# Who makes the input of each scan step: seven of sixteen by ScalarE, six by VectorE, three by GpSimd

## The chip, the core and the metric

The kernel runs on one core of a Trainium2 chip. A core has TensorE (matrix products and transposes, in the profile PE, its weight loads PEld), VectorE (DVE), ScalarE (ACT), GpSimd (POOL) and SyncE (SP, which here issues most DMAs). Each engine works through its own list of instructions in order, and semaphores tie the lists together. The metric is device microseconds (us) of one execution; lower is better. The time before is the median of three runs.

## The reference: what is computed

The input is `x` (4 images, 32 x 32 positions, 384 channels, float32). One block of a state space model with a mixture of experts behind it:

- `x` is normalised over channels and projected to `xh` and `z` (192 channels each); `xh` goes through a 3 x 3 depthwise convolution and SiLU.
- A selective scan runs over the 1024 positions in four directions `k` (rows, columns, both also backwards), for each of 16 states `n`:

```
dA = exp(d_t[..., None] * As)
h  = h * dA + (d_t * u_t)[..., None] * B_t[:, :, None, :]
y  = sum over n of h * C_t
```

- The four results are added, normalised, gated by `silu(z)`, projected back to 384 channels and added to `x`.
- Each token then goes through the one of 8 experts that its gate picks, and that result is added too.

The change is in the scan alone.

## The kernel before, in words

**Two passes.** The four images are handled as two pairs, one pass (`p`) each; partitions 0 to 63 hold one image of the pair, 64 to 127 the other, and the 192 channels lie in `CG` = 3 blocks `j`. A pass is: projection and convolution, the time steps `delta` and their products `du`, the scan, then norm, gate and output projection. The experts come after both passes.

**The scan.** A pass has `STEPS` = 128 steps: 4 directions, 2 halves of 512 positions, 16 states. Sixteen steps with one direction and one half are called a group here (8 groups a pass, g = 0 to 7), and a step is named by its state number n = 0 to 15 in its group. In even groups the recurrence starts from zero ("first half"); in odd groups ("second half") it starts from the state kept by the first half, which VectorE reads as a column. A step needs five things:

1. Its *input* `du * B` (128 x 1536, to a slot of the ring `X3` with `RING` = 7 slots). The letter `MAKER[n]` says who makes it. **P**: GpSimd, by one multiplication (L464). **D**: VectorE, by one multiplication that reads `du` from PSUM (L913), issued one step ahead: `input_of(s + 1)` stands before `scans(s)`. **A**: ScalarE scales the transposed `du` by columns of B, in eight small *scalings* (L683, 128 x 192 each, `scale_duT`), and TensorE transposes the result block by block into PSUM (L1273, `transpose_input`). When the eight scalings are issued is the table `SCALED`: the key is the step in which ScalarE issues them, `(m, f, l)` means scalings f to l - 1 of state m.
2. Its *decay* `exp(delta * A)`, three ScalarE instructions `exp(s, j)`. For a P or D step they go to one of only two PSUM banks `dA` (L706), taken in turn, so each waits until the scan before the last one has ended. For an A step they go to SBUF (L701, `dAs`), and the two banks hold the transposed input instead.
3. Three *scans* on VectorE (L937), one for each j.
4. The product with C on GpSimd (L479, in place in `X3`), which releases `s_hc`.
5. The sum over n on TensorE (L1247, `add_up`, three matrix products of 128 x 512 into PSUM), which frees the slot of `X3`. The first step of a group also opens the sums (L1236, `open_sums`), and for that the sums of the group before must have been taken away by ScalarE: `y_out` (L723 as one instruction, or L727 as three that also turn the block). It stands in step n = 2 of the next group.

**Order on ScalarE.** This is written out by hand, and the same for both kernels. In step s:

```python
exp(s, 0)
exp(s, 1)
...
if MAKER[n] == "A" or n % 2:
    exp(s, 2)
...
for m, f, l in todo:
    if m < STEPS:
        scale_duT(m, f, l)
if n == 2 and g:
    y_out(g - 1)
if not (MAKER[n] == "A" or n % 2):
    exp(s, 2)
```

So scalings and `y_out` stand in front of the third decay where n is even and the step is not A, and behind it otherwise. In first halves a 128 x 3 copy (L715, `keep_state`) is issued behind `exp(s, 1)` too. At n = 14 and 15 the `du` of the next group is copied out (L671, L691).

**Order on GpSimd.** In step s it makes the input of step s + 2 if that is a P step, and then multiplies step s by C.

**Loads.** SyncE loads the rows of B five steps ahead (for P and D steps only, ring of 4) and the rows of C six steps ahead (ring of 6). In step 4 x 16 of the first pass it also loads the next pass's images.

Of the kernel before, what the change touches and what calls it, by code (L numbers as in the profile page):

```python
# [10 lines left out]
ACT = mybir.ActivationFunctionType  # L11
AX_X = mybir.AxisListType.X

P = 128
NB, HH, WW, DM = 4, 32, 32, 384
L = HH * WW
DI, NS, R, ND = 192, 16, 24, 4
# [11 lines left out]
IN_ARENA = 5  # L29
RING, B_RING, C_RING = 7, 4, 6  # L30
GROUPS_OF_PAIR = 4 * 2
MAKER = "PDADPDADPDADPDAA"
BY_SCALAR = (2, 6, 10, 14, 15)
LAST_D = 13
SCALED = {15: ((2, 0, 3),), 0: ((2, 3, 8),), 2: ((6, 0, 2),), 4: ((6, 2, 8),), 6: ((10, 0, 5),),
          8: ((10, 5, 8), (14, 0, 3)), 10: ((14, 3, 8),), 12: ((15, 0, 6),), 13: ((15, 6, 8),)}
B_AHEAD = 5
LB = HALF // P
KORDER = (0, 2, 1, 3)
PREP = (0, 1, 2, 3)  # L40
# [9 lines left out]
def build(nc, x, w_in, conv_w, conv_b, w_xd, w_dt, bias_row, a_log, d_skip, ln_g, ln_b, w_out,  # L50
          w_gate, b_gate, w1, w2, w3, sel, ident_d, half_ones, tri_d, out):
    ctx = ExitStack()
    with ctx:
# [6 lines left out]
        def sems(*ns):  # L60
            return [sem(n) for n in ns]
# [68 lines left out]
        BT = carve(ND * TT * 2 * len(BY_SCALAR)).rearrange("p (k t b n) -> p k t b n", k=ND, t=TT, b=2)  # L130
# [44 lines left out]
        for at in (GL, xc_at):  # L175
# [76 lines left out]
        s_btps, s_bt, s_duTps, s_duT, s_scaled, s_dAs, s_inT = sems(  # L252
            "b_columns_in_psum", "b_columns_ready", "duT_in_psum", "duT_ready", "scaled_ready",
            "dA_in_sbuf", "input_in_psum")
# [22 lines left out]
        STEPS = ND * 2 * NS  # L277
# [6 lines left out]
        def inputs_before(c, maker):  # L284

            return c // NS * MAKER.count(maker) + MAKER[:c % NS].count(maker)

# [10 lines left out]
        def _(sp):  # L298
# [18 lines left out]
            for p in range(PAIRS):  # L317
# [30 lines left out]
                def load_b(s):  # L348
                    r = rows_before(STEPS * p + s)
                    before = [q for q in range(s) if MAKER[q % NS] != "A"]  # L350
                    if len(before) >= B_RING:
# [79 lines left out]
        def _(g):  # L431
# [5 lines left out]
            for p in range(PAIRS):  # L437
# [17 lines left out]
                def input_of(s):  # L455

                    _, gr, _, n, _ = place(s)
                    c = STEPS * p + s
                    g.wait_ge(s_steps[gr % 2], 32 * (GROUPS_OF_PAIR // 2 * p + gr // 2 + 1))
                    r = rows_before(c)  # L460
                    g.wait_ge(s_b[r % B_RING], 32 * (r // B_RING + 1))
                    if c >= RING:
                        g.wait_ge(s_xfree, c - RING + 1)
                    g.tensor_tensor(X3[c % RING], steps[gr % 2][1], Bs[r % B_RING][:, None, :].to_broadcast([P, CG, HALF]),  # L464
                                    ALU.mult).then_inc(s_dbp, 1)

                for s in range(STEPS):
                    kk, _, _, n, first = place(s)
                    c = STEPS * p + s
                    if s == 0:  # L470
                        input_of(0)
                    if s + 2 < STEPS and MAKER[(s + 2) % NS] == "P":
                        input_of(s + 2)
                    g.wait_ge(s_c[c % C_RING], 32 * (c // C_RING + 1))
                    g.wait_ge(s_scan, CG * (c + 1))
                    if first:
                        g.wait_ge(s_state, states_before(c + 1))
                    x = X3[c % RING]
                    g.tensor_tensor(x, x, Cs[c % C_RING][:, None, :].to_broadcast([P, CG, HALF]), ALU.mult)\  # L479
                     .then_inc(s_hc, 1)  # L480
# [53 lines left out]
        def _(a):  # L534
# [73 lines left out]
            for p in range(PAIRS):  # L608
# [7 lines left out]
                def b_columns(i):  # L616
                    c, cols = ND * p + i, bank[0].rearrange("p (t b n) -> p t b n", t=TT, b=4)[:, :, 0:2, :]
                    a.wait_ge(s_btps, c + 1)
                    a.activation(BT[:, PREP[i], :, :, 0:4], cols[:, :, :, 2:15:4], ACT.Copy)
                    a.activation(BT[:, PREP[i], :, :, 4], cols[:, :, :, 15], ACT.Copy).then_inc(s_bt, 1)  # L620

                if p:
                    a.wait_ge(s_tst, 16 * 2 * GROUPS)
# [900 lines left out]
```

## Time and profile before

| | |
|---|---|
| median of 3 runs | 1888.18 us (1885.74 to 1891.11) |
| the profiled execution | 1891.21 us, its span 1889.4 us |
| busy share of the span | PE 82%, PEld 40%, DVE 77%, ACT 57%, POOL 69% |
| scan of the first pass | 148.3 to about 710 us |
| scan of the second pass | 903.3 to about 1459 us |
| granted TensorE clock, mean | 0.918 |

The span is that from the first to the last instruction. Busy shares are means over stages that have different limits: in the two scan stretches VectorE and GpSimd are both nearly always busy, in the experts behind 1555 us TensorE is. A busy time of a group of instructions is the sum of their durations. Instructions of an engine overlap a little at their ends, so the distance from one start to the next (called the pitch below) is shorter than the duration.

### The profile page before, as it was taken

To read this page: it belongs to the slowest core of one execution; us is meant where nothing else is said; L and a number is where in the kernel's file an instruction comes from. 1 tells how busy PE (TensorE), PEld (TensorE's weight loads), DVE (VectorE), ACT (ScalarE), POOL (GpSimd) and SP (SyncE) were. 2 spreads that over 40 slices of the span, in tenths; PEclk is the share of its full clock that TensorE was granted. 3 is DMA by queue.
4 is the path that set the end of the run, shared out by engine and by line. 5 is a ranking of instruction groups with operands and counts; after the bars stand their busy time and mean duration, and the time that the engine had idled before them with its cause. 6 is when DMAs were issued, how large, how long until landed. Compare 5 with 4: busy or idle time off the path is not lost.

```text
span 1889.4 us, 17637 instructions
## 1 busy us (share of the span) xinstructions
PE 1542.0 (82%) x4977; PEld 764.8 (40%) x4978; DVE 1460.3 (77%) x1564; ACT 1080.5 (57%) x1959; POOL 1305.8 (69%) x498
## 2 busy tenths in 40 slices
PE   5866877886887887986688888888887659999997
PEld 2323433433433433442244344344343345555554
DVE  5588999998999997847899999999997762333322
ACT  3777777776777764657777777776775211111110
POOL 1458999998999992414899999999998112222222
PEclk9877999998999888987899999988999869999999
DMA  3184435436434312028443543443433471111110
GB/s 120 45 295 177 126 115 174 132 101 211 125 110 139 103 55 90 35 95 280 177 131 109 175 133 99 145 139 93 136 106 103 178 280 43 42 42 47 50 50 18
DMA packets 107232, 227.96 MB, mean 121 GB/s; under 512 B 18222, under 2 KB 31057, under 8 KB 103312
## 3 DMA queue, kind: packets, MB, share of 16 engines
q1 hardware_dynamic: 102160, 213.02, 34.3%
q0 software_dynamic: 4992, 14.01, 2.4%
q8 instruction: 33, 0.54, 0.1%
q14 instruction: 47, 0.39, 0.1%
HBM read 183.93 MB, written 44.40 MB: 121 GB/s over the span
## 4 chain that ended last, share of the span: by engine, by line
PE 33%; DVE 28%; POOL 18%; issue 13%; ACT 4%; DMA 3%; SPq 1%; DVEq 0%; POOLq 0%; ACTq 0%
DVE arena L937 18%; POOL arena L479 14%; PE psum L1400 10%; PE psum L1419 5%; DVE arena L913 4%; PE psum L1247 3%; PE psum L1220 2%; PE psum L1150 2%; POOL arena L464 2%; DMA arena<-bc_dram 2%; PE psum L1273 2%; PE psum L1326 1%; PE psum L1182 1%; PE psum L1345 1%; POOL arena L446 1%
## 5 line engine op out<-in xcount | busy, mean ns | idle before, releaser
L479 POOL TENSOR_TENSOR arena<-arena 128x1536 f32<-128x1536 f32 x256 | 875.8, 3452 | 31.7 <-ACT arena L715 19.1
L1247 PE MATMUL psum<-arena,ident 128*128 128x512 f32 x1536 | 742.0, 620 | 67.0 <-POOL arena L479 66.9
L937 DVE TENSOR_TENSOR_SCAN arena<-psum,arena 128x512 f32<-128x512 f32 x528 | 614.9, 1231 | 0.0
L706 ACT ACTIVATE psum<-arena 128x512 f32<-128x512 f32 x528 | 364.2, 690 | 271.0 <-DVE arena L937 259.1
L1247 PEld LDWEIGHTS psum<-arena,ident 128*128 128x128 f32 x1536 | 283.1, 198 | 371.0 <-issue 251.4
L937 DVE TENSOR_TENSOR_SCAN arena<-arena,psum 128x512 f32<-128x512 f32 x240 | 289.3, 1240 | 24.9 <-PE psum L1273 20.1
L1273 PE MATMUL psum<-ident,arena 128*128 128x128 f32 x960 | 159.8, 295 | 151.4 <-DVE arena L937 151.4
L1273 PEld LDWEIGHTS psum<-ident,arena 128*128 128x128 f32 x960 | 122.0, 151 | 289.1 <-issue 147.4
L683 ACT ACTIVATE arena<-arena 128x192 f32<-128x192 f32 x640 | 234.6, 440 | 0.0
L464 POOL TENSOR_TENSOR arena<-arena 128x1536 f32<-128x1536 f32 x64 | 220.6, 3447 | 4.5 <-issue 4.5
L913 DVE TENSOR_TENSOR arena<-psum,arena 128x1536 f32<-128x1536 f32 x112 | 194.2, 1734 | 24.0 <-ACT psum L691 13.8
L1400 PE MATMUL psum<-arena 128*128 x468 | 197.9, 560 | 0.0
L796 ACT ACTIVATE arena<-psum 128x384 f32<-128x384 f32 x39 | 19.1, 490 | 294.3 <-PE psum L1391 294.3
L701 ACT ACTIVATE arena<-arena 128x512 f32<-128x512 f32 x240 | 160.1, 709 | 10.5 <-DVE arena L937 9.9
L453 POOL TENSOR_TENSOR arena<-arena 128x1024 f32<-128x1024 f32 x24 | 63.1, 2627 | 133.1 <-DVE arena L900 133.1
L516 POOL TENSOR_TENSOR gap<-one 128x1 f32<-128x1 f32 x39 | 11.5, 296 | 206.1 <-DVE arena L1100 206.1
L1083 DVE TENSOR_TENSOR arena<-arena,psum 128x469 f32<-128x469 f32 x39 | 25.1, 644 | 120.0 <-ACT arena L801 111.1
L1400 PEld LDWEIGHTS psum<-arena 128*128 128x128 f32 x468 | 86.4, 191 | 74.9 <-issue 65.0
L1419 PE MATMUL psum<-arena 128*128 (+1 forms) x312 | 107.3, 487 | 1.0 <-DVE arena L1090 1.0
L895 DVE SCALAR_TENSOR_TENSOR arena<-arena 128x1024 f32<-128x1024 f32 x24 | 43.2, 1799 | 54.7 <-ACT arena L641 54.5
L1220 PE MATMUL psum<-arena 64*128 64x512 f32 x96 | 62.7, 800 | 20.4 <-ACT arena L632 18.6
L446 POOL TENSOR_TENSOR arena<-arena 128x1024 f32<-128x1024 f32 x16 | 38.0, 2374 | 55.6 <-ACT arena L576 53.6
(161 smaller groups left out, 1464.2 us busy)
## 6 DMA issues: line engine op xcount, KB each, us to landing
arena<-bc_dram SPq DMA_DIRECT2D x864, 128.0 KB, 3.0
step_dram<-arena SPq DMA_DIRECT2D x16, 1536.0 KB, 8.1
arena<-step_dram SPq DMA_DIRECT2D x32, 768.0 KB, 8.0
arena<-in_x SPq DMA_DIRECT2D x8, 1536.0 KB, 9.4
arena<-in_w SPq DMA_DIRECT2D x6, 1876.0 KB, 10.7
t_dram<-arena SPq DMA_DIRECT2D x16, 386.0 KB, 3.8
arena<-in_w SPq DMA_DIRECT2D x4, 1536.0 KB, 13.6
z_dram<-arena SPq DMA_DIRECT2D x2, 1536.0 KB, 5.2
```

The lines of the kernel that those rows point to most:

```text
L464: g.tensor_tensor(X3[c % RING], steps[gr % 2][1], Bs[r % B_RING][:, None, :].to_broadcast([P, CG, HALF]), ALU.mult).then_inc(s_dbp, 1)
L479: g.tensor_tensor(x, x, Cs[c % C_RING][:, None, :].to_broadcast([P, CG, HALF]), ALU.mult)\
L683: a.activation(blocks(scaled[index % 2])[:, :, k, b, :], blocks(duT)[:, :, k, b, :], ACT.Copy, scale=BT[:, kk, LB * half + k, b, BY_SCALAR ...
L701: a.activation(dAs[j], steps[g % 2][0][:, j, :], ACT.Exp, scale=A[:, KORDER[kk], j, n:n + 1]).then_inc(s_dAs, 1)
L706: a.activation(dA[e % 2], steps[g % 2][0][:, j, :], ACT.Exp, scale=A[:, KORDER[kk], j, n:n + 1]).then_inc(s_dA, 1)
L913: v.tensor_tensor(X3[c % RING], dups, Bs[r % B_RING][:, None, :].to_broadcast([P, CG, HALF]), ALU.mult).then_inc(s_dbv, 1)
L937: v.tensor_tensor_scan(x, decay, given, 0.0 if first else state[:, n, j:j + 1], ALU.mult, ALU.add).then_inc(s_scan, 1)
L1220: ins = pe.matmul(bank[2 + 2 * j + h], wdt[0:64, KORDER[PREP[i]], j, :], xd[i % 2][0:64, h * HALF:(h + 1) * HALF], start=True, stop=True)
L1247: ins = pe.matmul(bank[j], ident[:, :], X3[c % RING][:, j, :], start=False, stop=(n == NS - 1), skip_group_check=True)
L1273: ins = pe.transpose(dA[e % 2][:, k * P:(k + 1) * P], scaled[index % 2][:, at:at + P], ident[:, :])
L1400: ins = pe.matmul(bk[:, 0:F], xsT[u][:, k, :], w[:, k, bass.ds(e * F, F)], start=(k == 0), stop=(k == KC - 1))
L1419: ins = pe.matmul(bank[6 + u][:, 0:DM], hidT[u][0:m, k, :], W3[0:m, k, bass.ds(e * DM, DM)], start=(k == 0), stop=(k == FC - 1))
```

## The change

The string that says who makes each input, the table of ScalarE's scalings and the step in which GpSimd begins its inputs:

```diff
-MAKER = "PDADPDADPDADPDAA"
-BY_SCALAR = (2, 6, 10, 14, 15)
+MAKER = "PDDADADAPADAPDAA"
+BY_SCALAR = (3, 5, 7, 9, 11, 14, 15)
 LAST_D = 13
-SCALED = {15: ((2, 0, 3),), 0: ((2, 3, 8),), 2: ((6, 0, 2),), 4: ((6, 2, 8),), 6: ((10, 0, 5),),
-          8: ((10, 5, 8), (14, 0, 3)), 10: ((14, 3, 8),), 12: ((15, 0, 6),), 13: ((15, 6, 8),)}
+SCALED = {15: ((3, 0, 3),), 0: ((3, 3, 8),), 1: ((5, 0, 8),), 4: ((7, 0, 3),), 5: ((7, 3, 8),),
+          6: ((9, 0, 3),), 7: ((9, 3, 6),), 8: ((9, 6, 8),), 9: ((11, 0, 7),), 10: ((11, 7, 8), (14, 0, 2)),
+          11: ((14, 2, 5),), 12: ((14, 5, 8), (15, 0, 4)), 13: ((15, 4, 8),)}
@@ (GpSimd)
-                    if s + 2 < STEPS and MAKER[(s + 2) % NS] == "P":
-                        input_of(s + 2)
+                    if s + 3 < STEPS and MAKER[(s + 3) % NS] == "P":
+                        input_of(s + 3)
@@ (ScalarE, columns of B for the A steps)
-                    a.activation(BT[:, PREP[i], :, :, 0:4], cols[:, :, :, 2:15:4], ACT.Copy)
-                    a.activation(BT[:, PREP[i], :, :, 4], cols[:, :, :, 15], ACT.Copy).then_inc(s_bt, 1)
+                    a.activation(BT[:, PREP[i], :, :, 0:5], cols[:, :, :, 3:12:2], ACT.Copy)
+                    a.activation(BT[:, PREP[i], :, :, 5:7], cols[:, :, :, 14:16], ACT.Copy).then_inc(s_bt, 1)
```

In a group of 16 steps there were 4 P, 7 D and 5 A steps; now there are 3 P, 6 D and 7 A.

ScalarE's list, from the last step of group 0 to step 4 of group 1 (a second half). Before, L683 are the scalings, L706 the decays of P and D steps, L701 those of A steps, L723 is `y_out`:

```order
L683 ACTIVATE arena<-arena 128x3x64 x3
L706 ACTIVATE psum<-arena 128x512 x2
L715 ACTIVATE arena<-arena 128x3
L683 ACTIVATE arena<-arena 128x3x64 x5
L706 ACTIVATE psum<-arena 128x512 x4
L701 ACTIVATE arena<-arena 128x512 x3
L683 ACTIVATE arena<-arena 128x3x64 x2
L723 ACTIVATE arena<-psum 128x3x512
L706 ACTIVATE psum<-arena 128x512 x5
L683 ACTIVATE arena<-arena 128x3x64 x6
```

And in the change, where all these stand one line later in the file (L684 for L683, and so on):

```order
L684 ACTIVATE arena<-arena 128x3x64 x3
L707 ACTIVATE psum<-arena 128x512 x2
L716 ACTIVATE arena<-arena 128x3
L684 ACTIVATE arena<-arena 128x3x64 x5
L707 ACTIVATE psum<-arena 128x512 x4
L684 ACTIVATE arena<-arena 128x3x64 x8
L707 ACTIVATE psum<-arena 128x512 x2
L724 ACTIVATE arena<-psum 128x3x512
L707 ACTIVATE psum<-arena 128x512
L702 ACTIVATE arena<-arena 128x512 x3
L707 ACTIVATE psum<-arena 128x512 x2
L684 ACTIVATE arena<-arena 128x3x64 x3
```

Behind the last decay of step 1 there now stand eight scalings ahead of the first decay of step 2, `y_out` stands ahead of a decay of the same P or D step where it stood behind those of an A step, and in step 4 three scalings stand ahead of the last decay.

VectorE's list at the same place, from step 14 of group 0 on (order prints a scan as SCALAR_TENSOR_TENSOR; L937 are scans and L913 are inputs). Before:

```order
L937 SCALAR_TENSOR_TENSOR arena<-arena,psum 128x512 x6
L913 TENSOR_TENSOR arena<-psum,arena 128x1536
L937 SCALAR_TENSOR_TENSOR arena<-psum,arena 128x512 x6
L913 TENSOR_TENSOR arena<-psum,arena 128x1536
L937 SCALAR_TENSOR_TENSOR arena<-arena,psum 128x512 x3
L937 SCALAR_TENSOR_TENSOR arena<-psum,arena 128x512 x3
```

In the change:

```order
L938 SCALAR_TENSOR_TENSOR arena<-arena,psum 128x512 x6
L914 TENSOR_TENSOR arena<-psum,arena 128x1536
L938 SCALAR_TENSOR_TENSOR arena<-psum,arena 128x512 x3
L914 TENSOR_TENSOR arena<-psum,arena 128x1536
L938 SCALAR_TENSOR_TENSOR arena<-psum,arena 128x512 x6
L914 TENSOR_TENSOR arena<-psum,arena 128x1536
L938 SCALAR_TENSOR_TENSOR arena<-arena,psum 128x512 x3
```

The inputs of steps 1 and 2 now stand ahead of the scans of steps 0 and 1, and the scans of steps 1 and 2 follow one another with nothing between.

## Rows read from the trace of the kernel before

**Rows 1.** Chain that ended last, the page's line by source line.
```profile
DVE arena L937 18%; POOL arena L479 14%; PE psum L1400 10%; PE psum L1419 5%; DVE arena L913 4%; PE psum L1247 3%; PE psum L1220 2%; PE psum L1150 2%; POOL arena L464 2%; DMA arena<-bc_dram 2%; PE psum L1273 2%; PE psum L1326 1%; PE psum L1182 1%; PE psum L1345 1%; POOL arena L446 1%
```
**Rows 2.** Windows: the first pass's scan; length, then busy time of each engine.
```profile
148.30:707.00 558.70, 448.42 (x1365) 216.03 (x1366) 537.81 (x441) 408.67 (x794) 538.52 (x159) 0.94 0.40 128
```
**Rows 3.** Timeline of POOL: start, length, line, count.
```profile
548.02 13.73 POOL L479 TENSOR_TENSOR arena<-arena 128x1536 f32<-128x1536 f32 x4
561.71 3.45 POOL L464 TENSOR_TENSOR arena<-arena 128x1536 f32<-128x1536 f32 x1
```
**Rows 4.** Timeline of DVE, a first half, then a second half.
```profile
565.54 1.73 DVE L913 TENSOR_TENSOR arena<-psum,arena 128x1536 f32<-128x1536 f32 x1
567.19 6.79 DVE L937 TENSOR_TENSOR_SCAN arena<-psum,arena 128x512 f32<-128x512 f32 x6
573.89 1.73 DVE L913 TENSOR_TENSOR arena<-psum,arena 128x1536 f32<-128x1536 f32 x1
...
663.04 3.62 DVE L937 TENSOR_TENSOR_SCAN arena<-arena,psum 128x512 f32<-128x512 f32 x3
666.58 3.61 DVE L937 TENSOR_TENSOR_SCAN arena<-psum,arena 128x512 f32<-128x512 f32 x3
670.10 1.74 DVE L913 TENSOR_TENSOR arena<-psum,arena 128x1536 f32<-128x1536 f32 x1
```
**Rows 5.** Timeline of DVE: where groups begin, and the first pass's last scans.
```profile
216.10 1.73 DVE L913 TENSOR_TENSOR arena<-psum,arena 128x1536 f32<-128x1536 f32 x1
284.55 1.73 DVE L913 TENSOR_TENSOR arena<-psum,arena 128x1536 f32<-128x1536 f32 x1
701.64 5.17 DVE L937 TENSOR_TENSOR_SCAN arena<-arena,psum 128x512 f32<-128x512 f32 x4 [0.81 <-ACT arena L701]
903.31 1.76 DVE L913 TENSOR_TENSOR arena<-psum,arena 128x1536 f32<-128x1536 f32 x1 [7.66 <-ACT psum L691]
969.51 1.73 DVE L913 TENSOR_TENSOR arena<-psum,arena 128x1536 f32<-128x1536 f32 x1
```
**Rows 6.** What DVE's scans (L937), then its inputs (L913), waited for.
```profile
  PE psum L1273: 20.1, 21
  ACT arena L701: 1.9, 3
...
  issue: 10.2, 3
```
**Rows 7.** Timeline of ACT: chained decays, six scalings, decays again.
```profile
568.43 0.69 ACT L706 ACTIVATE psum<-arena 128x512 f32<-128x512 f32 x1 [0.32 <-DVE arena L937]
...
582.98 0.19 ACT L715 ACTIVATE arena<-arena 128x3 f32<-128x3 f32 x1
583.08 2.17 ACT L683 ACTIVATE arena<-arena 128x192 f32<-128x192 f32 x6
585.15 0.67 ACT L706 ACTIVATE psum<-arena 128x512 f32<-128x512 f32 x1
```
**Rows 8.** Timeline of ACT: step 13, two scalings, then step 14's decays; `y_out`.
```profile
431.96 2.83 ACT L727 ACTIVATE arena<-psum 128x512 f32<-128x512 f32 x3
434.59 0.69 ACT L706 ACTIVATE psum<-arena 128x512 f32<-128x512 f32 x1
...
555.83 0.69 ACT L706 ACTIVATE psum<-arena 128x512 f32<-128x512 f32 x1 [0.48 <-DVE arena L937]
556.46 0.79 ACT L683 ACTIVATE arena<-arena 128x192 f32<-128x192 f32 x2
557.15 1.93 ACT L701 ACTIVATE arena<-arena 128x512 f32<-128x512 f32 x3
...
575.43 1.43 ACT L723 ACTIVATE arena<-psum 128x1536 f32<-128x1536 f32 x1
700.87 0.72 ACT L701 ACTIVATE arena<-arena 128x512 f32<-128x512 f32 x1 [1.27 <-DVE arena L937]
```
**Rows 9.** The page's group of TensorE's transposes for A steps: busy, mean | idle before.
```profile
L1273 PE MATMUL psum<-ident,arena 128*128 128x128 f32 x960 | 159.8, 295 | 151.4 <-DVE arena L937 151.4
```

## The prediction

> **What bounds the kernel now.** I read the chain of waits first. Of the span, 18% lie on VectorE's scans, 14% on GpSimd's products with C and 4% on VectorE's inputs [rows 1]: the chain passes through the scan stage, changing between these two engines, and nothing outside that stage is touched by the change. The windows say how full they are: of the first pass's 558.7 us VectorE is busy 537.8, GpSimd 538.5, TensorE 448.4 and ScalarE 408.7 [rows 2]. Two engines at 96% are a tie, so I went to the timelines for the pitch of each.
>
> GpSimd: four products take 13.69 us from start to start [rows 3], 3.42 each, an input the same. A group has 16 + 4 of them, 68.4 us. VectorE: six scans take 6.70 us in a first half (1.117 each), three take 3.52 in a second half (1.175), and an input moves the next scan by 1.65 [rows 4]. Undisturbed groups last 66.2 us (first half, from 903.31 to 969.51) and 68.45 (second half, from 216.10 to 284.55) [rows 5]. So two groups are 134.65 us on VectorE and 136.8 on GpSimd: GpSimd is slightly the slower, falls behind, and what depends on it (TensorE's sums, behind which the transposes for A steps queue) then stops VectorE now and then. That is the 20.1 us of waits for transposes, with 1.9 for decays. Another 10.2 us are "issue" waits before VectorE's inputs [rows 6], where the list waits for rows of B; I leave these as they are, since SyncE still issues them five steps ahead.
>
> The third view is ScalarE's timeline, and it decides the forecast. It is busy only 73% of the stage, but it is in lockstep with VectorE: a decay for a P or D step may start only when the scan that used its bank has ended. The first scan starts at 567.19 and the next one 1.117 later at 568.31, and the decay starts at 568.43 [rows 4, 7]: 0.12 us behind the start of the following scan. A decay is 0.69 long, the next ScalarE instruction can start 0.63 behind its start [rows 8], and from the end of a late decay (700.87 + 0.72) to the scan that waited for it (701.64) are 0.05 us [rows 5, 8]. So a decay that starts at 0.12, ends at 0.81 and may be followed by its scan at 0.86 is due at 1.117: 0.26 us in hand, and no lead can be built up over P and D steps. What ScalarE does between two such decays is free only up to its gap.
>
> **The change, part by part.**
>
> *Removed.* One VectorE input a group: 16 groups x 1.65 = 26.4 us off VectorE. One GpSimd input a group: 16 x 3.42 = 54.7 us off GpSimd, which then needs 38 x 3.42 = 130.0 us for two groups, less than VectorE's 134.65 - 3.30 = 131.35 even with no stall. So GpSimd no longer falls behind, and the 22.0 us of waits [rows 6] mostly go: of 24 such waits I keep a tenth, 2 us. Beginning an input three steps ahead moves it in front of one product; with GpSimd faster than VectorE this is worth nothing. It reaches the slot of the ring freed by step s - 4, whose sum TensorE has made by then.
>
> *Added.* Two A steps a group. On TensorE 24 transposes, at their full 295 ns [rows 9] 7.1 us, where TensorE has (558.7 - 448.4) / 8 = 13.8 us idle: nothing. On ScalarE 16 scalings of 0.345 us (six in 2.07) [rows 7], 5.5 us a group, 88 us in all, while (558.7 - 408.7) / 8 = 18.8 us a group are idle. By the sum they fit. By their places they don't. Each place worked out, with zero at the scan start named, p = 1.117 in first halves and 1.175 in second halves, and `keep_state` costing 0.10 in first halves only [rows 7]:
>
> - **Step 1, eight scalings behind its third decay.** From the second scan of step 1: 0.12 + 0.63 + 8 x 0.345 + 0.69 + 0.05 = 4.25 us until step 2 can be scanned. VectorE is there after two scans, at 2.23 or 2.35, because the input of step 2 was already made ahead of the scans of step 1. Stall 2.02 or 1.90 us.
> - **Steps 4, 6, 10, three scalings between second and third decay.** From the step's first scan: 0.12 + 0.63 + (0.10) + 1.04 + 0.69 + 0.05 = 2.63 or 2.53, due at 2.23 or 2.35. Stall 0.40 or 0.18, three times. Before, every P or D step of even n had a VectorE input in front (1.65 more), so that six scalings fitted: 3.66 against 3.88; the row shows the decay straight behind its six, at 585.15 [rows 7]. Now an A step follows, and there is none.
> - **Step 8**, two scalings: 2.28 against 2.23, 0.05 in first halves. **Step 12**, seven, with an input in front: 4.01 against 3.88, 0.13 in first halves.
> - **Step 13, four behind the third decay**, ahead of step 14: 0.12 + 0.63 + 1.38 + 0.71 + 0.05 = 2.89, stall 0.66 or 0.54. With two scalings, as now, the same sum gives 2.20 and fits; the rows show those two between decay and decay [rows 8].
>
> That is 4.06 us in a first half and 2.98 in a second, 8 x 7.04 = 56.3 us.
>
> - **`y_out` in step 2.** It now lies ahead of the third decay of a D step. Continuing from the stall of step 1, the decays of step 2 start at 3.51 and 4.14, `y_out` at 4.77 (4.87). As one instruction it takes 1.37 (1.43 less the overlap), as three 2.63 (431.96 to 434.59) [rows 8]. The third decay then allows its scan at 6.88 (6.98) or 8.14 (8.24), due 4.25 + 2p = 6.60 (6.48). Stalls, g = 1 to 7: 0.28, 0.50, 1.54, 1.76, 0.28, 0.50, 1.54: 6.4 a pass, 12.8 us in all. The sums of the new group open behind it and step 3's transposes queue behind those, but the input of step 4 (1.65 us) covers that.
>
> *Sum.* 69.1 - 26.4 - 22.0 + 2.0 = +22.7 us. Against its own 1891.2 us the profiled execution would be 1913.9; it stands 3 us above the median of the runs, 1888.2, so I forecast **1911 us**.
>
> The Trainium skill ("Perfetto Trace Analysis", section "Optimizing Scalar/DVE Operations") says that with VectorE saturated, moving some of its work to ScalarE may pay; by busy shares alone that speaks for this change. It is the second rival below. The same page calls occupancy the way to find the engine to optimise; here the engine at 73% is the one that I expect to set the pace.
>
> **Rivals.**
>
> 1. *The busy sum holds (ends faster).* If ScalarE hid all its scalings, VectorE would be left with -26.4 and the waits for transposes with -20: 1888.2 - 46.4, about 1842 us. For it: 18.8 us idle a group against 5.5 added. Against it: that idle time is in pieces of 0.42 us behind each decay [rows 7] and longer ones at A steps. It decides where the stalls are under 46.4 / 16 = 2.9 us a group; I work out 4.3. Chance 0.08.
> 2. *Only the long bursts cost.* If the short ones at steps 4, 6, 8, 10, 12, 13 (56.3 - 8 x 3.92 = 25 us together) fall in slack that I have put too low, the sum is -2 us: 1886. Chance 0.12, about evenly faster and same.
> 3. *The waits for transposes stay.* With seven A steps VectorE depends on TensorE at 7 of 16 steps, and a sum issued ahead of a transpose still waits for GpSimd; keeping all 20 us gives 1931. Against it: GpSimd is the slack engine then. Chance 0.10.
> 4. *My forecast*, 1898 to 1925 by itself (the short stalls halved; or half the old waits kept). Chance 0.70.
>
> The range runs from between rival 2 and the baseline, 1886, to rival 3, 1931; outside are rival 1 and tails. No change within 0.3% (about 6 us, what a measurement of this kernel can tell) gets 0.09, faster 0.11, slower 0.80.
>
> **What the new profile would show.** VectorE waiting about 70 us for ScalarE's decays (L707, and L702 at step 14) where it now waits 1.9 for them; a gap of about 2 us ahead of the first scan of every step 2; a second one in that step, 0.3 to 1.8 us, from g = 1 on; groups of about 69 to 71 us; GpSimd with idle time in every group, waiting for scans. VectorE's inputs 96 instead of 112, GpSimd's 48 instead of 64, scalings 896 instead of 640. I am wrong if the first scan of step 2 follows step 1 without a gap, or if the waits for transposes are still near 20 us.

## The result

The change makes the kernel slower: 1965.13 us (median of 4 runs, 1964.41 to 1967.81) against 1886.96 us (4 runs, 1885.29 to 1891.11), a ratio of 1.042 [1.040, 1.043]. I had said slower, but 1911 us, range 1886 to 1931. The profiled execution took 1964.71 us with a span of 1962.8; before, the span was 1889.4. So 73.4 us have to be found.

The chain of the changed kernel, the page's line by source line, answers to [rows 1]:

```profile
DVE arena L938 27%; PE psum L1401 9%; PE psum L1420 5%; DVE arena L914 5%; ACT arena L684 4%; PE psum L1237 4%; PE psum L1248 3%; PE psum L1274 2%; PE psum L1221 2%; PE psum L1151 2%; ACT psum L707 2%; PE psum L1183 1%; PE psum L1327 1%; ACT arena L728 1%; PE psum L1346 1%
```

GpSimd's products, 14% of the chain before, have left it (all of GpSimd is 1% of it now). New are ScalarE's scalings (L684, 4%), its turned `y_out` (L728) and, what I had not expected, TensorE's opening products (L1237, 4%).

The page's groups of costly instructions; behind the bar busy time, mean ns of one, then idle time ahead of them with its main releaser:

```profile
L480 POOL TENSOR_TENSOR arena<-arena 128x1536 f32<-128x1536 f32 x256 | 875.9, 3454 | 166.8 <-ACT arena L716 90.3
L1248 PE MATMUL psum<-arena,ident 128*128 128x512 f32 x1536 | 740.3, 604 | 68.5 <-POOL arena L480 68.2
...
L684 ACT ACTIVATE arena<-arena 128x192 f32<-128x192 f32 x896 | 329.1, 440 | 0.0
L1274 PE MATMUL psum<-ident,arena 128*128 128x128 f32 x1344 | 207.9, 279 | 115.0 <-DVE arena L938 115.0
...
L914 DVE TENSOR_TENSOR arena<-psum,arena 128x1536 f32<-128x1536 f32 x96 | 166.3, 1732 | 15.0 <-ACT psum L692 15.0
L465 POOL TENSOR_TENSOR arena<-arena 128x1536 f32<-128x1536 f32 x48 | 165.8, 3455 | 0.0
```

The counts are those announced: 96 inputs by VectorE, 48 by GpSimd, 896 scalings. The second row holds what undid the forecast: `add_up` issues three products for each of 256 steps, 768 in all, and the profile has 1536 records of them. So a float32 product of 128 x 512 is **two** records in the profile (a record is one instruction as the trace lists it).

What VectorE's scans (L938) waited for, in us and times; it answers to [rows 6]:

```profile
  PE psum L1274: 72.2, 16
  ACT psum L707: 46.3, 50
  ACT arena L702: 9.8, 16
```

The waits for transposes went from 20.1 to 72.2 us, those for decays from 1.9 to 56.1; the 10.2 us of "issue" waits ahead of VectorE's inputs are gone (L914 still has 15.0 us of idle time, two waits at the start of a pass; L913 had the same two, 13.8 us, one of them in [rows 5]). With the 26.4 us of removed inputs that is 52.1 + 54.2 - 10.2 - 26.4 = 69.7 of the 73.4 us. Most of the rest lies in late scans that the rows count as busy time. In a second half of the change:

```profile
249.40 3.76 DVE L938 TENSOR_TENSOR_SCAN arena<-psum,arena 128x512 f32<-128x512 f32 x3
...
256.59 3.61 DVE L938 TENSOR_TENSOR_SCAN arena<-psum,arena 128x512 f32<-128x512 f32 x3
```

Step 6 has three scalings ahead of its last decay, step 8 two; step 6 is 0.15 us longer. Three such steps in 8 groups are 3.6 us.

Of the 72.2 us, 70.3 lie in 14 waits at one place, the first scan of step 3 in every group but the first of a pass. The timelines of VectorE, TensorE and ScalarE there, g = 1 (start, length, engine, line, count, in brackets the idle time before and what ended it; TensorE's last two rows are the same place in g = 2):

```profile
227.69 3.74 DVE L938 TENSOR_TENSOR_SCAN arena<-psum,arena 128x512 f32<-128x512 f32 x3 [1.88 <-ACT psum L707]
231.35 1.73 DVE L914 TENSOR_TENSOR arena<-psum,arena 128x1536 f32<-128x1536 f32 x1
...
236.99 3.62 DVE L938 TENSOR_TENSOR_SCAN arena<-arena,psum 128x512 f32<-128x512 f32 x3 [3.91 <-PE psum L1274]
```

```profile
229.59 4.25 PE L1237 MATMUL psum<-arena 128*128 128x512 f32 x6 [3.33 <-ACT arena L724]
...
233.68 2.74 PE L1248 MATMUL psum<-arena,ident 128*128 128x512 f32 x6
...
236.25 1.04 PE L1274 MATMUL psum<-ident,arena 128*128 128x128 f32 x8
...
303.18 5.00 PE L1237 MATMUL psum<-arena,ident 128*128 128x512 f32 x6 [4.72 <-ACT arena L724]
308.02 2.74 PE L1248 MATMUL psum<-arena,ident 128*128 128x512 f32 x6
```

```profile
224.12 2.86 ACT L684 ACTIVATE arena<-arena 128x192 f32<-128x192 f32 x8
...
226.88 1.28 ACT L707 ACTIVATE psum<-arena 128x512 f32<-128x512 f32 x2
...
228.11 1.43 ACT L724 ACTIVATE arena<-psum 128x1536 f32<-128x1536 f32 x1
```

Read them from below. The eight scalings hold up step 2's decays (VectorE waits 1.88), and `y_out` comes behind these. At its end, 229.5, TensorE may open the new sums (three products, six records), then it adds step 0 (three more), and only then, at 236.25, come the transposes for step 3. VectorE was ready at 231.35 + 1.73 = 233.08 and waits 3.91 us.

Two things make the queue long. The sums take 2.57 us for three products, 0.86 each (233.68 to 236.25), where I had reckoned 0.43. And the opening products take 4.09 (4.84 in g = 2), for the same number of the same size. The windows say why; columns are length, busy time of PE, PEld, DVE, ACT and POOL, granted clock, DMA share and GB/s:

```profile
229.60:231.60 2.00, 2.00 (x3) 0.97 (x4) 2.00 (x3) 2.00 (x4) 0.56 (x2) 0.50 0.68 140
303.20:308.00 4.80, 4.80 (x6) 2.02 (x7) 3.16 (x3) 2.59 (x5) 4.80 (x2) 0.55 0.92 323
308.00:311.00 3.00, 3.00 (x11) 1.50 (x10) 0.00 (x0) 0.00 (x0) 0.80 (x1) 1.00 0.97 312
```

TensorE had been idle for 3.33 us ahead of the first window (4.72 ahead of the second) and was granted half the clock, 1.2 GHz, for most of the opening products; for the sums behind them in g = 2 (the third window) it was back at 2.4 GHz.

The same sum can be made for each of the 14 places, from the starts in the three timelines. Six products at full clock (5.14 us) would leave waits of 2.38 to 2.73 us, 34.7 in all; the other 35.6 of the 70.3 us are time by which the queue was longer than that, the low clock. Three products' time, 2.57 us, would leave between -0.19 and 0.16, that is nothing.

The experiments were made from these rows. VectorE's scans and ScalarE's decays keep their line numbers in all that start from the changed kernel; TensorE's lines move by a few in some.

### The profile page after: what moved, and what is told of

The parts are those of the page before. It is cut to its first block, busy times and chain, and to the rows that moved or that the text cites. A ratio compares the mean times of both kernels' runs of the same rounds, so it can differ in the third digit from the quotient of the medians.

```text
span 1962.8 us, 18725 instructions
## 1 busy us (share of the span) xinstructions
PE 1590.3 (81%) x5361; PEld 781.5 (40%) x5362; DVE 1440.0 (73%) x1548; ACT 1150.8 (59%) x2215; POOL 1252.3 (64%) x482
## 4 chain that ended last, share of the span: by engine, by line
PE 37%; DVE 37%; ACT 12%; issue 12%; POOL 1%; DMA 1%; DVEq 0%; ACTq 0%; POOLq 0%
DVE arena L938 27%; PE psum L1401 9%; PE psum L1420 5%; DVE arena L914 5%; ACT arena L684 4%; PE psum L1237 4%; PE psum L1248 3%; PE psum L1274 2%; PE psum L1221 2%; PE psum L1151 2%; ACT psum L707 2%; PE psum L1183 1%; PE psum L1327 1%; ACT arena L728 1%; PE psum L1346 1%
## 5 line engine op out<-in xcount | busy, mean ns | idle before, releaser
L480 POOL TENSOR_TENSOR arena<-arena 128x1536 f32<-128x1536 f32 x256 | 875.9, 3454 | 166.8 <-ACT arena L716 90.3
L1248 PE MATMUL psum<-arena,ident 128*128 128x512 f32 x1536 | 740.3, 604 | 68.5 <-POOL arena L480 68.2
L938 DVE TENSOR_TENSOR_SCAN arena<-psum,arena 128x512 f32<-128x512 f32 x432 | 514.0, 1235 | 47.6 <-ACT psum L707 46.3
L707 ACT ACTIVATE psum<-arena 128x512 f32<-128x512 f32 x432 | 293.8, 685 | 300.4 <-DVE arena L938 288.2
L938 DVE TENSOR_TENSOR_SCAN arena<-arena,psum 128x512 f32<-128x512 f32 x336 | 397.3, 1232 | 84.0 <-PE psum L1274 72.2
L684 ACT ACTIVATE arena<-arena 128x192 f32<-128x192 f32 x896 | 329.1, 440 | 0.0
L1274 PE MATMUL psum<-ident,arena 128*128 128x128 f32 x1344 | 207.9, 279 | 115.0 <-DVE arena L938 115.0
L1274 PEld LDWEIGHTS psum<-ident,arena 128*128 128x128 f32 x1344 | 154.4, 142 | 311.8 <-DVE arena L938 163.7
L702 ACT ACTIVATE arena<-arena 128x512 f32<-128x512 f32 x336 | 223.0, 708 | 5.0 <-DVE arena L938 4.6
L914 DVE TENSOR_TENSOR arena<-psum,arena 128x1536 f32<-128x1536 f32 x96 | 166.3, 1732 | 15.0 <-ACT psum L692 15.0
L465 POOL TENSOR_TENSOR arena<-arena 128x1536 f32<-128x1536 f32 x48 | 165.8, 3455 | 0.0
L454 POOL TENSOR_TENSOR arena<-arena 128x1024 f32<-128x1024 f32 x24 | 63.1, 2628 | 131.3 <-DVE arena L901 131.3
L1237 PE MATMUL psum<-arena,ident 128*128 128x512 f32 x72 | 63.8, 1056 | 56.2 <-ACT arena L728 30.4
```

What stands on the lines that cost most here:

```text
L684: a.activation(blocks(scaled[index % 2])[:, :, k, b, :], blocks(duT)[:, :, k, b, :], ACT.Copy, scale=BT[:, kk, LB * half + k, b, BY_SCALAR ...
L702: a.activation(dAs[j], steps[g % 2][0][:, j, :], ACT.Exp, scale=A[:, KORDER[kk], j, n:n + 1]).then_inc(s_dAs, 1)
L707: a.activation(dA[e % 2], steps[g % 2][0][:, j, :], ACT.Exp, scale=A[:, KORDER[kk], j, n:n + 1]).then_inc(s_dA, 1)
L914: v.tensor_tensor(X3[c % RING], dups, Bs[r % B_RING][:, None, :].to_broadcast([P, CG, HALF]), ALU.mult).then_inc(s_dbv, 1)
L938: v.tensor_tensor_scan(x, decay, given, 0.0 if first else state[:, n, j:j + 1], ALU.mult, ALU.add).then_inc(s_scan, 1)
L1237: pe.matmul(bank[j], lhs, src[:, j, cs], start=True, stop=False, skip_group_check=True)
```

## The experiments

### One item of the queue, the burst, and both

TensorE adds step 0 in step 2, ahead of step 3's transposes. The first experiment puts it behind them, with the opening products, which the code issues ahead of step 0's sums:

```diff
-                        behind = 3 if more and n > 2 else 2
+                        behind = 3 if more and n > 1 else 2
```

> The change, but TensorE adds step 0 of a group only behind the transposes of step 3 (and not ahead of them). Theory A (the transposes of step 3 queue on TensorE behind y_out, the three opening products and the sums of step 0): the 14 waits of 3.9 to 5.4 us ahead of the scans of step 3 go, about -66 us of the change's 1965, so 1900 (1895 to 1910), and the waits for decays stay at about 56 us. Rival B (ScalarE's burst of eight scalings causes both waits by itself): the stall at step 3 moves to another step, 1950 to 1965.

Measured: 1955.86 us (1954.65 to 1957.11), ratio to before 1.036 [1.033, 1.039], 9 us under the change. The expectation missed by 56 us; the number is in the range of rival B, a wait that moves to another step. (The cause that B names, the burst by itself, doesn't hold by the next run, for which B had 1870.) Step 3 was free; step 5 was not (VectorE and TensorE, g = 1):

```profile
241.00 4.24 PE L1237 MATMUL psum<-arena 128*128 128x512 f32 x6
245.07 5.31 PE L1248 MATMUL psum<-arena,ident 128*128 128x512 f32 x12
...
250.22 0.60 PE L1274 MATMUL psum<-ident,arena 128*128 128x128 f32 x4
...
250.95 1.28 DVE L938 TENSOR_TENSOR_SCAN arena<-arena,psum 128x512 f32<-128x512 f32 x1 [3.03 <-PE psum L1274]
```

Nine products now stand between the transposes of step 3 and those of step 5, 9.2 us, with the opening ones again at 4.07 for three. The waits for transposes are 53.2 us in 25 places instead of 72.2 in 16, those for decays are unchanged (46.3 and 10.6). Shifting the queue to the next pair of A steps moved the wait with it.

The second moves the eight scalings of step 1 to step 3, where they follow the three decays of an A step, which do not use the two PSUM banks and so need not wait for a scan of the same step:

```diff
-SCALED = {15: ((3, 0, 3),), 0: ((3, 3, 8),), 1: ((5, 0, 8),), 4: ((7, 0, 3),), 5: ((7, 3, 8),),
+SCALED = {15: ((3, 0, 3),), 0: ((3, 3, 8),), 3: ((5, 0, 8),), 4: ((7, 0, 3),), 5: ((7, 3, 8),),
```

> The change, but the eight scalings of state 5 are issued in step 3 (an A step with a VectorE input ahead of its scans) and not in step 1. Theory A: only the 16 waits of 1.9 to 2.0 us ahead of step 2 go, -31 us; the queue on TensorE moves with y_out and its stall stays near 4.5 us a group, so 1934 (1928 to 1940). Rival B: both go, 1870.

Measured: 1922.59 us (1921.66 to 1925.38), ratio 1.018 [1.015, 1.021], 42.5 us under the change and 11 under the expectation, which had left step 3's wait as it was. What the scans waited for:

```profile
  PE psum L1274: 52.3, 18
  ACT psum L707: 20.3, 38
```

Decays give back 26.0 us, and the transposes another 19.9, since `y_out` is earlier and TensorE, g = 1, idle for less ahead of it:

```profile
226.65 2.84 PE L1237 MATMUL psum<-arena 128*128 128x512 f32 x6 [1.69 <-ACT arena L724]
...
231.91 1.04 PE L1274 MATMUL psum<-ident,arena 128*128 128x128 f32 x8
...
232.64 3.62 DVE L938 TENSOR_TENSOR_SCAN arena<-arena,psum 128x512 f32<-128x512 f32 x3 [2.49 <-PE psum L1274]
```

```profile
226.70:229.30 2.60, 2.60 (x6) 1.20 (x7) 2.24 (x3) 2.60 (x6) 2.60 (x2) 1.00 0.54 156
```

Here the opening products ran at the full clock, as in 7 of the 14 groups. Six products take 5.26 us, and the wait that is left, 2.49, is the double count by itself. From the rows of the change I get the same: 229.59 + 6 x 0.857 + 0.74 (first transpose to scan) = 235.47, less 233.08 is 2.39. The other 1.52 us of the 3.91 there are the clock. Over the 14 places the clock's part falls from 35.6 to 14.6 us by this edit, and the part of the count stays at 34.6. So a part of the clock's cost goes with the burst, and a part doesn't.

The third does both:

> The change with both edits (sums of step 0 behind the transposes of step 3, scalings of state 5 in step 3). Theory A: the two are added, -66 -31, 1868 (1860 to 1880), faster than the kernel before. Rival B: as with the burst moved alone, 1870 too, so this run tells A from B only beside the other two; what it tests is whether the distribution 3 P, 6 D, 7 A can win at all.

Measured: 1933.21 us (1932.37 to 1934.53), ratio 1.024 [1.021, 1.027]: slower than the burst alone, by 11 us, and 65 above the expectation. Step 5 waits 3.41 us in g = 1, and the waits for transposes (54.8 us in 26 places) are as large as in the first experiment. In these two runs the rows of the opening products are 3.75 us or longer in every group, where they are 2.74 at full clock, and the mean granted clock is 0.905 and 0.907, where the change has 0.928 and the burst moved alone 0.936. So the burst is one cause. The new place of the sums gives 9 us without the burst moved and costs 11 with it: it is no remedy.

### GpSimd two steps ahead, and three ahead in the kernel before

I had put beginning GpSimd's inputs a step earlier at nothing. Two runs test that. The first undoes it in the change, the second makes it alone in the kernel before:

```diff
-                    if s + 3 < STEPS and MAKER[(s + 3) % NS] == "P":
-                        input_of(s + 3)
+                    if s + 2 < STEPS and MAKER[(s + 2) % NS] == "P":
+                        input_of(s + 2)
```

> The change, but GpSimd begins its inputs two steps ahead, as before. If the earlier start is worth nothing while GpSimd is the engine with time to spare: 1965 within 3 us. Rival: it was needed for the two P steps 8 and 12 that follow A steps, then a wait of VectorE for inputs appears, 5 us or more slower.

Measured: 2009.96 us (2006.51 to 2010.8), ratio 1.064 [1.060, 1.067], 44.8 us above the change, where no difference was expected; the rival named beside it, a wait of VectorE for inputs, does appear, but as only 6.8 us in 8 places. GpSimd in g = 0, first in the change, then in the experiment, with two rows of VectorE behind it:

```profile
168.84 6.85 POOL L480 TENSOR_TENSOR arena<-arena 128x1536 f32<-128x1536 f32 x2 [1.82 <-ACT arena L716]
175.65 3.45 POOL L465 TENSOR_TENSOR arena<-arena 128x1536 f32<-128x1536 f32 x1
179.04 13.67 POOL L480 TENSOR_TENSOR arena<-arena 128x1536 f32<-128x1536 f32 x4
```

```profile
178.64 3.45 POOL L480 TENSOR_TENSOR arena<-arena 128x1536 f32<-128x1536 f32 x1 [1.86 <-ACT arena L716]
...
182.05 3.44 POOL L465 TENSOR_TENSOR arena<-arena 128x1536 f32<-128x1536 f32 x1
185.45 13.66 POOL L480 TENSOR_TENSOR arena<-arena 128x1536 f32<-128x1536 f32 x4
...
185.52 3.45 DVE L938 TENSOR_TENSOR_SCAN arena<-psum,arena 128x512 f32<-128x512 f32 x3 [0.85 <-POOL arena L465]
...
212.30 7.68 DVE L938 TENSOR_TENSOR_SCAN arena<-arena,psum 128x512 f32<-128x512 f32 x6 [2.65 <-PE psum L1274]
```

In the change GpSimd makes step 8's input at 175.65, in time that it would otherwise spend waiting; in the experiment it idles 1.86 us, waiting for the scans of step 5, and makes the input afterwards, too late for VectorE (0.85). From 182.05 on it has no gap up to step 14, so the delay stays: its products are late, TensorE's sums with them, and the transposes of step 14, in the queue behind those sums, too (2.65). The clock has a part here as well: TensorE waited 2.64 us for the product of step 11 and then took 4.30 us for three products instead of 2.68. Waits for transposes are 107.4 us instead of 72.2. GpSimd has 166.8 us of idle time in the change and still carries 45 us of this difference: it has time to spare by its sum, but not in the second half of each group.

In the kernel before:

```diff
-                    if s + 2 < STEPS and MAKER[(s + 2) % NS] == "P":
-                        input_of(s + 2)
+                    if s + 3 < STEPS and MAKER[(s + 3) % NS] == "P":
+                        input_of(s + 3)
```

> The kernel before, with GpSimd beginning its inputs three steps ahead instead of two and nothing else. In the change the earlier start was worth 45 us, because it filled time in which GpSimd waited in step 5 or 6. Theory C: before, GpSimd has hardly any idle time to fill (it is the slower of the two engines), so 1886 within 5 us. Rival: it shortens the waits for transposes at steps 14 and 15 here too, 5 to 20 us faster.

Measured: 1907.97 us (1901.95 to 1911.45) against 1888.69, ratio 1.009 [1.007, 1.012]: slower, where I had expected no difference. VectorE's inputs (L913) there:

```profile
  issue: 30.8, 12
```

In [rows 6] these were 10.2 us in 3. GpSimd's inputs (L464) waited 36.3 us for "issue", also in 12 places, where they had waited 4.5. The rows name no releaser, but the page's chain by line does:

```profile
POOL arena L479 15%; DMA arena<-bc_dram 10%; PE psum L1400 10%; POOL arena L464 9%; SPq L346 6%; PE psum L1419 5%; DVE arena L937 4%; PE psum L1150 3%; PE psum L1220 2%; PE psum L1326 1%; PE psum L1182 1%; PE psum L1345 1%; PE psum L1247 1%; PE psum L1410 1%; DVE arena L913 1%
```

`bc_dram` holds the rows of B and C; their loads were 2% of the chain in [rows 1]. The 12 waits of each engine are one in each of groups 1 to 6 of both passes, the groups in which SyncE puts the load of the next group's steps (2 x 768 KB) ahead of those rows:

```profile
233.90 1.22 SPq L340 DMA_DIRECT2D arena<-step_dram  x2
...
245.18 3.43 POOL L464 TENSOR_TENSOR arena<-arena 128x1536 f32<-128x1536 f32 x1 [2.29 <-issue]
```

In g = 1 that load is issued at 233.90, in the kernel before at 230.50, and the rows loaded from 234 to 247 us take a median of 6.0 us to land, against 3.2 over the whole execution; GpSimd wants its row a step earlier. So the waits are for rows of B, late behind the load of steps. No run moved that load, so how much of the 19 us is due to it isn't tested.

### Without the opening products

The three opening products are left out, so the output lacks the skip term and the sums of earlier directions; step 0 of each group opens its bank itself:

```diff
-                    for j in range(CG):
-                        lhs, src = (skipw[:, j, :], xc3) if kk == 0 else (ident[:, :], y3 if kk == 1 else yT3)
-                        pe.matmul(bank[j], lhs, src[:, j, cs], start=True, stop=False, skip_group_check=True)
...
-                                    start=False, stop=(n == NS - 1), skip_group_check=True)
+                                    start=(n == 0), stop=(n == NS - 1), skip_group_check=True)
```

> The change without the three products that open the sums of a group (the skip term and the sums of the groups before are left out of the output; the wait for y_out stays). Theory A with each product taking two records of 0.43 us: step 3's wait falls by the opening products' 2.6 us at full clock, by 14 x 2.6 = 36 us, to about 1929; the half-rate clock that the rows show in the opening products behind TensorE's idle time then falls on the sums of step 0 instead. If the clock were a matter of these products alone, their whole 4.1 to 5.0 us would go: 14 x 4.7, 1900.

Measured: 1930.22 us (1922.73 to 1935.25), ratio 1.023 [1.021, 1.025], within 2 us of the expectation (the profiled execution was the shortest of the four). Waits for transposes fall from 72.2 to 29.2 us, those for decays stay (46.2 and 9.1). What is left at step 3 shows that the low clock belongs to the place and not to the opening products. TensorE, g = 2:

```profile
300.54 5.26 PE L1245 MATMUL psum<-arena,ident 128*128 128x512 f32 x6 [4.75 <-ACT arena L724]
305.63 1.04 PE L1271 MATMUL psum<-ident,arena 128*128 128x128 f32 x8
```

Now step 0's sums stand first behind the idle time, and it is they that take 5.09 us instead of 2.57. The queue has three products here, 2.57 us at full clock, which step 4's input would cover; the 26.8 us that the 14 places still wait are the clock alone.

### Can the same shares of work be placed better?

If the places are the cause, other places should win back the 73 us with the same `MAKER`. The first try: scalings spread so that none outruns its gap, `y_out` behind the third decay of step 2, the opening products between the transposes of step 3's second and third block, step 0's sums behind them:

```diff
-SCALED = {15: ((3, 0, 3),), 0: ((3, 3, 8),), 1: ((5, 0, 8),), 4: ((7, 0, 3),), 5: ((7, 3, 8),),
-          6: ((9, 0, 3),), 7: ((9, 3, 6),), 8: ((9, 6, 8),), 9: ((11, 0, 7),), 10: ((11, 7, 8), (14, 0, 2)),
-          11: ((14, 2, 5),), 12: ((14, 5, 8), (15, 0, 4)), 13: ((15, 4, 8),)}
+SCALED = {15: ((3, 0, 3),), 0: ((3, 3, 8),), 1: ((5, 0, 2),), 3: ((5, 2, 8),), 5: ((7, 0, 8),),
+          6: ((9, 0, 1),), 7: ((9, 1, 6),), 8: ((9, 6, 8),), 9: ((11, 0, 8),), 10: ((14, 0, 1),),
+          11: ((14, 1, 6),), 12: ((14, 6, 8), (15, 0, 4)), 13: ((15, 4, 6),), 14: ((15, 6, 8),)}
...
-                    if n == 2 and g:
-                        y_out(g - 1)
                     if not (MAKER[n] == "A" or n % 2):
                         exp(s, 2)
+                    if n == 2 and g:
+                        y_out(g - 1)
...
+                            if n == 3 and j == 1:
+                                open_sums(s - n)
...
-                        behind = 3 if more and n > 2 else 2
+                        behind = 3 if more and n > 1 else 2
```

> The change's distribution (3 P, 6 D, 7 A, three ahead) with all queues rearranged: scalings moved to the places that fit (at most 1 or 2 where an uncovered decay follows, 6 to 8 behind the decays of A steps with a VectorE input next), y_out behind the third decay of step 2, the opening products between the second and third transpose block of step 3, sums of step 0 behind that step's transposes. Theory A (order on the queues is what costs, not the distribution): waits of VectorE under 25 us, 1852 (1840 to 1875), faster than before. Rival D (seven A steps load TensorE and ScalarE beyond what the lockstep allows): 1885 or slower.

Measured: 1887.92 us (12 runs, 1885.47 to 1892.02), ratio 1.000 [0.9985, 1.001]. 77 us are won back, all of the loss and nothing more; the 1852 us of the expectation missed by 36. The waits for transposes are 39.6 us, of which 25.6 lie at one new place, the third scan of step 3 behind the opening products. TensorE and VectorE, g = 1:

```profile
231.24 3.98 PE L1237 MATMUL psum<-arena 128*128 128x512 f32 x6
...
235.76 1.28 DVE L938 TENSOR_TENSOR_SCAN arena<-arena,psum 128x512 f32<-128x512 f32 x1 [1.48 <-PE psum L1270]
```

In the two groups in which those products took 2.74 us, at full clock, this wait is missing. The second takes the new table alone:

> The change with the table of scalings of the rearranged kernel and nothing else. The waits for decays at steps 2, 4, 6, 10, 14 go (56 us in the change, here about 10, those of y_out staying); step 3's wait for transposes stays at about 50 us as where only the burst was moved: 1922 - 15 = 1905.

Measured: 1921.96 us (1920.39 to 1925.12), ratio 1.017 [1.015, 1.019], 17 above the expectation. Decays cost 15.8 us instead of 56.1, but the waits for transposes stay at 65.1. The table is worth 43 us and the order on TensorE and of `y_out`, put on top of it, 34. Moving the eight scalings of step 1 alone had given 42.5 of those 43: taking away the short stalls too brought nothing, since the waits for transposes are 12.8 us longer than there.

The third starts from the first and also spreads the opening products: one ahead of the third block of step 3, two behind it, and step 1's sums behind step 5's transposes:

```diff
+                            if n == 3 and j:
+                                open_sums(s - n, (0,) if j == 1 else (1, 2))
...
-                        behind = 3 if more and n > 2 else 2
+                        behind = 3 if n == 3 or more and n > 1 else 2
```

> The rearranged kernel, but only the first of the three opening products stands ahead of the third transpose block of step 3, and the sums of step 1 are left until behind the first transposes of step 5. The rearranged kernel's wait of 1.3 to 2.2 us ahead of the third scan of step 3, in 14 groups, goes (21 us). Theory E: with it GpSimd's idle time behind that stall shrinks by as much, so that the whole group is shorter by it: 1888 - 20 = 1868. Rival F: the opening products and the sums are only moved, and step 5 waits for them instead (as where the sums of step 0 alone were moved): 1885 to 1895.

Measured: 1881.04 us (12 runs, 1875.4 to 1887.52) against 1886.52 (17 runs), ratio 0.997 [0.996, 0.998]. This is the fastest version, 5.5 us under the kernel before; the interval leaves out 1, but the size is at the limit of what can be told. The expectations were 1868 and, for the rival, 1885 to 1895, and it lies between them. The scans still wait:

```profile
  PE psum L1270: 27.9, 29
  ACT arena L702: 6.4, 15
```

The last moves a P step of the third version from 8 to 4, `MAKER = "PDDAPADADADAPDAA"`, with a table to suit, so that GpSimd has an input to make early in the group:

> As the kernel with one opening product ahead, and GpSimd's second input is that of step 4 instead of step 8 (VectorE makes that of 8; scalings adapted). GpSimd's list is full from step 4 to 15 and has 3 to 7 us idle in steps 0 to 3 of a group. Theory G (the place of GpSimd's inputs matters, not their number): the input of step 4, begun in step 1, falls into that idle time, worth up to 3.4 us a group, less 0.6 (1.9 behind a turned y_out) for the missing cover at step 3: about -30 against the kernel with one opening product, 1840. Rival H: step 3 without an input ahead of its scans brings the wait for transposes back: 1870 or slower.

Measured: 1894.09 us (6 runs, 1890.28 to 1896.35), ratio 1.004 [1.002, 1.005], 54 above the expectation and slower than the third. The waits for transposes stay (26.6 us), and those for A steps' decays (L702) rise from 6.4 to 21.5.

## Why the prediction was off, point by point

The prediction's sum with the terms as measured is 56.1 + 3.6 (decays) + 72.2 (transposes) - 26.4 (inputs) - 22.0 (old waits) - 10.2 (issue waits) = 73.3 us, where it had 22.7. The stalls on ScalarE's side are there, but nearly all of the loss is a wait that the prediction put at nothing: without its 70.3 us the terms come to +3.0, which can't be told from no change. That the kernel came out slower, as said, is therefore luck in good part.

- **ScalarE's stalls: right in kind and place, somewhat too high.** I said 69.1 us, the rows show 56.1, and 3.6 more in lengthened scans. Step 2: 1.97 and 1.88 us (said 2.02 and 1.90). Step 14: 0.60 to 0.62 (0.66 and 0.54). `y_out`: 0 to 0.25 as one instruction, 1.24 to 1.52 as three (0.28, 0.50, 1.54, 1.76), 9.0 us together for 12.8. The short ones of steps 4, 6 and 10 in first halves: 0.27 (0.40). Part of the difference is only bookkeeping: an idle time in these rows begins at the end of the instruction before, and my sums ran from start to start, where instructions overlap by 0.08 us.
- **VectorE's inputs: right.** 96 of them at 1.65 us, 26.4 us less.
- **Waits for transposes, -22 + 2: wrong, and this is the step that failed.** The old ones mostly went: outside step 3 two are left, 1.9 us. That GpSimd's lag was their cause fits (making its inputs late brought 35 us of waits back), but wasn't tested in the kernel before. The failure is a new term. The prediction says of `y_out`: "The sums of the new group open behind it and step 3's transposes queue behind those, but the input of step 4 (1.65 us) covers that." It does so only at half the true length. I had taken a record of 0.43 us for a product, a figure that the prediction doesn't print, so the queue came to 2.6 us; six products are 5.14, and at the two places shown the first three take 4.09 and 4.84 instead of 2.57, since the clock is low. For g = 1: by my count the scan could start at 229.59 + 2.58 + 0.74 = 232.91, before VectorE is ready (233.08); with the count set right it waits 2.39, and with the clock 3.91. In 14 groups the term is 70.3 us where I had zero. The count is 34.7 of it and the low clock 35.6, of which moving the burst of scalings took 21 away.
  The Trainium skill ("FP8 and Floating Point Precision", section "TensorE Precision Notes") has a true FP32 product as four passes through the array. By that rule 512 columns at 2.4 GHz are an estimated 4 x 512 / 2400 = 0.85 us; the trace agrees with its 0.86 a product. Of the clock, the Trainium skill ("TensorE: Matmul & The Clock Gate", section "Why this matters for your kernels") warns of idle gaps between bursts of products as bringing the lower level back; the windows above agree, 0.50 and 0.55 behind such gaps, 1.00 behind 1.69 us.
- **The signs named in advance.** The gap of about 2 us ahead of every step 2 is there. The waits for transposes, near 20 us of which were named as a sign of being wrong, are 72.2. Group 1 lasts 73.7 us (215.35 to 289.08) instead of 69 to 71.
- **Why the kernel before had none of it.** There step 2 is an A step. Its transposes stand ahead of the opening products, and the next A step is step 6, four steps away. Its opening products come as 2.74 to 2.84 us of work, at the full clock, in 11 of 16 groups; g = 2:

```profile
296.31 2.74 PE L1236 MATMUL psum<-arena,ident 128*128 128x512 f32 x6
298.88 1.45 PE L1247 MATMUL psum<-arena,ident 128*128 128x512 f32 x3
```

  The new `MAKER` puts A at 3 and 5 and leaves step 2 a D step, so the same code issues both opening products and step 0's sums ahead of transposes. I had followed what the new letters do to ScalarE's and VectorE's lists, and not to TensorE's.
- **The issue waits, left at 10.2: wrong in our favour.** None are left in the change.
- **"Three steps ahead is worth nothing": wrong.** It is worth 44.8 us in the change and costs 19 in the kernel before. I had compared sums over two groups, and GpSimd's work isn't even within one.
- **Rivals.** The first, the busy sum, didn't hold, nor the second, only the long bursts: the short stalls show as 6.5 us at steps 4, 6 and 10, 9.8 at step 14 and 3.6 as lengthened scans, 19.9 of the 25. But with the long burst moved, taking most of them away too won nothing, so their rows say more than they cost there. The third had the right kind of wait, kept at 20 us by GpSimd's lag; it was a new wait, 3.5 times as large.

What stays open is why the rearranged versions stop at the old time. By its rows the first of them saves 26.4 us of inputs and 7.4 of issue waits; it gives back 19.5 us in waits for transposes, 1.8 in waits for decays and 5.1 in longer scans. That leaves 7.4 us, and the span is 2.9 us shorter; the rest of the difference I can't place. What is left of these waits at step 3 is the low clock. Whether GpSimd, idle in a group's first steps and nearly without a gap behind them, would hold VectorE up if they went too, I didn't separate.

## What to carry to other kernels

When a table decides who makes what, follow its effect on every engine's list, above all on the one that seems to have time to spare (TensorE here, which the prediction had as idle for 13.8 us a group): a queue of 5 us ahead of one needed transpose delays it whatever the engine does in the rest of the group. Check what one record stands for, by its count against the program's loops, before a pitch is used as a price. And a stall upstream may be paid twice, once as a wait and once because TensorE, left idle by it, may come back at half its clock: moving the burst gave back 26.0 us of the first kind and 19.9 of the second.

## What the runs showed of the hardware

- A float32 product of 128 x 512 on TensorE is two records, 0.86 us in all at 2.4 GHz (six records in 2.57 us, 1536 records for 768 products).
- Behind 3.33 and 4.72 us without work TensorE ran at 1.2 GHz (granted clock 0.50 and 0.55), and three such products took 4.09 and 4.84 us; behind 1.69 us they took 2.68 at a granted clock of 1.00. The idle time just ahead doesn't decide it alone: with the burst moved, behind 2.97 to 3.00 us three groups of eight took 2.68 and five took 4.06 to 4.38. Step 0's sums, put there in the run without opening products, took 5.09.
- GpSimd's 128 x 1536 product has a mean of 3.45 to 3.46 us in all versions, whether VectorE was stopped often or rarely.
